# VectorE's chained stages in pieces of one link, and scores over 32 rows at a time, in a two-layer gated stack

## The reference, cut to what matters

```
# x: 16 batches x 256 tokens x 256;  ctx: 16 x 120 x 256
x = x + tanh(g_xattn[0]) * attention_1(layernorm(x), ctx, mask)   # A: 4 heads of 64, rotary
x = x + tanh(g_ffn[0])   * ffn_fp4(layernorm(x))                  # F: blockwise FP4 of input and hidden
x = x + tanh(g_xattn[1]) * attention_2(layernorm(x), ctx, ctx)    # B: 16 heads of 16
x = x + tanh(g_ffn[1])   * moe(layernorm(x))                      # R routes each token to 2 of 8 experts, M runs them

# attention_2, for each batch and head (d_k = 16):
Q, K, V = query @ Wq + bq, key @ Wk + bk, value @ Wv + bv
attn = softmax(Q @ K.T / sqrt(16));  out = concat(attn @ V) @ Wo + bo

# fp4_quant_dequant, for blocks of 16 values:
scale = max(max(|x|) / 6, 1e-12);  q = nearest value of the FP4 grid to x / scale, times scale
```

## Time and profile before

| | us |
|---|---|
| median of 3 runs | 1640.79 |
| lowest, highest | 1635.14, 1644.37 |
| the profiled execution | 1642.42 |
| its span in the trace | 1640.8 |
| PE busy (share of the span) | 1400.4 (85%) |
| DVE busy | 1117.3 (68%) |
| ACT busy | 993.4 (61%) |
| POOL busy | 413.3 (25%) |
| mean granted TensorE clock, share of full speed | 0.949 |

### The profile page before, as it was taken

One profiled execution on the slowest core, in us unless ns is written; L12 is line 12 of the kernel. 1 busy time (PEld: TensorE's weight loads), 2 busy tenths in 40 slices (PEclk: granted clock), 3 DMA queues, 4 the chain that ended last, 5 costly groups with the idle time before them and its releaser, 6 DMA issues.

```text
span 1640.8 us, 35711 instructions
## 1 busy us (share of the span) xinstructions
PE 1400.4 (85%) x11645; PEld 1072.6 (65%) x11646; DVE 1117.3 (68%) x2887; ACT 993.4 (61%) x2861; POOL 413.3 (25%) x560
## 2 busy tenths in 40 slices
PE   2567789989999889989998671999999999999994
PEld 1445556665666566656664430888888888888883
DVE  7977779899988999899986534344444454444452
ACT  1244778888888888888876760444445444455542
POOL 0101011211122211212111112334433444344442
PEclk9587999999999999999999975999999999999997
DMA  6020132112320223203220005551231412322214
GB/s 192 13 87 30 62 103 103 45 61 104 103 92 21 95 104 103 72 33 104 94 94 8 8 14 179 177 162 32 33 112 30 114 32 35 108 35 32 35 31 123
DMA packets 63158, 123.58 MB, mean 75 GB/s; under 512 B 13955, under 2 KB 51967, under 8 KB 58879
## 3 DMA queue, kind: packets, MB, share of 16 engines
q1 hardware_dynamic: 45743, 102.75, 18.0%
q0 software_dynamic: 17312, 19.56, 7.2%
HBM read 78.64 MB, written 48.04 MB: 77 GB/s over the span
## 4 chain that ended last, share of the span: by engine, by line
PE 52%; DVE 32%; ACT 8%; issue 5%; DMA 2%; POOL 1%; SPq 0%; DVEq 0%; ACTq 0%; POOLq 0%
PE bank L1401 15%; PE bank L1403 14%; PE bank L1402 14%; DVE b_mn L1121 4%; ACT b_ex L746 3%; PE bank L1483 2%; PE bank L1495 2%; DVE wm L1238 1%; DVE f_hs L1182 1%; DVE split_room L1265 1%; DVE wm L1190 1%; PE bank L1719 1%; DVE x L1176 1%; DVE wm L1196 1%; DVE wm L1201 1%
## 5 line engine op out<-in xcount | busy, mean ns | idle before, releaser
L1401 PE MATMUL bank<-split_room,wm 128*128 128x256 f16 x1152 | 314.9, 273 | 8.2 <-issue 6.8
L1378 DVE SCALAR_TENSOR_TENSOR split_room<-bank,b12e,split_room 128x256 f32<-128x256 f32 x288 | 138.2, 484 | 265.6 <-ACT split_room L900 260.8
L1402 PE MATMUL bank<-split_room,wm 128*128 128x256 f16 x1152 | 314.8, 273 | 0.0
L1403 PE MATMUL bank<-split_room,wm 128*128 128x256 f16 x1152 | 314.7, 273 | 0.0
L900 ACT ACTIVATE split_room<-bank,b12e 128x256 f32<-128x256 f32 x288 | 134.2, 470 | 196.0 <-PE bank L1403 194.2
L746 ACT ACTIVATE b_ex<-bank,b_mn 128x120 f32<-128x120 f32 x512 | 177.0, 361 | 36.9 <-DVE b_mn L1121 28.0
L1403 PE MATMUL bank<-wm,split_room 128*128 128x256 f16 x576 | 157.0, 273 | 0.0
L1401 PE MATMUL bank<-wm,split_room 128*128 128x256 f16 x576 | 157.0, 273 | 0.0
L1402 PE MATMUL bank<-wm,split_room 128*128 128x256 f16 x576 | 157.0, 273 | 0.0
L692 POOL DMA_INDIRECT acc<-split_room,m_cur x72 | 116.1, 1612 | 133.0 <-ACT split_room L914 106.1
L1483 PE MATMUL bank<-b_k,b_q 128*128 128x480 f32 x256 | 131.8, 597 | 14.6 <-ACT b_q L834 14.6
(11 more groups left out here) (356 smaller groups left out, 3616.3 us busy)
## 6 DMA issues: line engine op xcount, KB each, us to landing
split_room<-in_L_ffn_W SPq DMA_DIRECT2D x48, 512.0 KB, 8.0
wsplit<-split_room SPq DMA_DIRECT2D x16, 1536.0 KB, 6.6
wm<-wsplit SPq DMA_DIRECT2D x16, 1536.0 KB, 8.5
acc<-x SPq DMA_DIRECT2D x17, 256.0 KB, 2.2
xin<-in_x SPq DMA_DIRECT2D x16, 256.0 KB
rows<-r_row SPq DMA_DIRECT2D x16, 256.0 KB, 3.7
ct<-in_ctx SPq DMA_DIRECT2D x16, 120.0 KB
cb<-in_ctx SPq DMA_DIRECT2D x16, 120.0 KB, 2.6
```

Source lines behind the costliest of these rows:

```text
L1378: dve.scalar_tensor_tensor(m_h[:, c % 3], bank[c % 4][:, TILE:2 * TILE], b12e[:, p, 1, c:c + 1], m_s[:, c % 2], ALU.add, ALU.mult).then_in ...
L1401: pe.matmul(o, lh, rh, start=start, stop=False)
L1402: pe.matmul(o, ll, rh, start=False, stop=False)
L1403: return pe.matmul(o, lh, rl, start=False, stop=stop)
```

## The change

1. **DVE's stages are cut at the waits.** `A.ln` becomes `A.ln`, `A.ln_1`, `A.ln_2`, `A.ln_3`; `F.ln`, `B.ln` and `R.ln` become three pieces each, `A.rk`, `A.r0`, `A.r1`, `A.p0` and `A.p1` two each, the FP4 stages eight per part instead of four (three for the input), `R.logit` six, `R.rank` seven. The instructions and their waits stay; the order decides what runs between two pieces.
2. **The scores of B** are made for two rounds at once. Each round is two products over the 32 rows of its group, 240 columns each (`e` is 0 and 1); the four products of two rounds lie in turn over two row groups and two banks. Both rounds may start only when the exponentials of the round before them are done, and the minimum of either waits for both. `b_k` shrinks to `[P, NK, 2, S]`, and ACT writes it with two copies over 128 partitions instead of eight over 32.
3. **For the new place of the heads**, the columns of `wq1`, `wk1` and the bias of the keys are split in eight (four) parts by DVE once, and the bias of the queries is loaded with 8 DMAs instead of 1.
4. **All tables of the order are new.**

```diff
-        b_k = sb("b_k", [P, NK, 2, QUAD, S])
+        b_k = sb("b_k", [P, NK, 2, S])
...
-            sp.dma_start(bqk[:, :], bq.rearrange("(c p) -> p c", p=P), allow_slow_non_contiguous=True).then_inc(wB_in, 16)
+            b_ = bq.rearrange("(c e f a d) -> d c e f a", c=2, e=2, f=2, a=2)
+            for c in range(2):
+                for a in range(2):
+                    for f in range(2):
+                        at = 64 * a + 32 * c + 16 * f
+                        sp.dma_start(bqk[at:at + K1, :], b_[:, c, :, f, a], allow_slow_non_contiguous=True).then_inc(wB_in, 16)
...
-                for j in range(QUAD):
-                    h = slice(PITCH * j, PITCH * (j + 1))
-                    for a in range(2):
-                        last = act.activation(b_k[h, :, a, j], bank[2][h, 0:NK * S].rearrange("p (c s) -> p c s", c=NK), ACT.Copy, scale=C[h, C_M + a:C_M + a + 1])
+                for f in range(2):
+                    last = act.activation(b_k[:, :, f], bank[2][:, 0:NK * S].rearrange("p (c s) -> p c s", c=NK), ACT.Copy, scale=C[:, C_M + f:C_M + f + 1])
...
+                        for c in range(2):
+                            for a in range(2):
+                                for k in range(NK):
+                                    k_ = slice(k, k + 1)
+                                    split(head_order(st1[:, n_ - 1, k_], c, a, True)[:, 0],
+                                          head_order(w[:, 0, k_], c, a, False)[:, 0], head_order(w[:, 1, k_], c, a, False)[:, 0])
...
-                        dve.wait_ge(G.s_mm, b * n + k + 1)
+                        dve.wait_ge(G.s_mm, b * n + (k + 1 if G is A else k // 2 * 2 + 2))
...
+                def pair(b, k0):
+                    if k0 == 0:
+                        pe.wait_ge(B.q, b + 1)
+                        pe.wait_ge(B.k, b + 1)
+                    else:
+                        pe.wait_ge(B.exp, b * n + k0)
+                    for e in range(NK):
+                        for k in (k0, k0 + 1):
+                            t, r = k // per, k % per
+                            h = slice(PITCH * r, PITCH * (r + 1))
+                            last = pe.matmul(sbks[k % 2][:, e * 2 * S:(e + 1) * 2 * S], q[h, e, t * P:(t + 1) * P], kk[h, e], start=True, stop=True)
+                            if e == NK - 1:
+                                last.then_inc(B.s_mm, 1)
...
-                            r = k % per
-                            last = pe.matmul(sbk[:, 0:QUAD * S], q[:, r % 2, t * P:(t + 1) * P], kk[:, r % 2, r // 2], start=True, stop=True)
```

DVE's steady order after the change:

```diff
+            "DVE": ("W1/1 A.ot/0 B.ln/2 B.rx1/3 W2/1 F.gu0/1 A.out/0 A.ln/-1 B.ln_1/2 A.ln_1/-1 B.ln_2/2 F.gu1/1 A.ln_2/-1 B.p7/3 "
+                "F.q0a/1 A.ln_3/-1 B.o1/3 F.q0a_1/1 F.q0a_2/1 F.gu2/1 B.out/3 R.ln/3 R.ln_1/3 R.ln_2/3 B.ct/2 B.zt/2 F.gu3/1 "
+                "F.q0b/1 F.q1a/1 F.q1a_1/1 F.q1a_2/1 F.q0c/1 F.q0c_1/1 B.v/2 A.t/-1 B.s0/2 B.s1/2 F.p0/1 R.t/3 F.p0_1/1 "
+                "F.q1b/1 A.rk/-1 R.logit/3 R.logit_1/3 R.logit_2/3 R.logit_3/3 R.logit_4/3 R.logit_5/3 F.q1c/1 B.s2/2 "
+                "R.rank_0/3 F.q1c_1/1 R.rank_1/3 F.p1/1 B.s3/2 F.p1_1/1 F.ht0/1 A.rk_1/-1 A.r0/-1 A.r0_1/-1 A.r1/-1 A.r1_1/-1 "
+                "B.s4/2 F.ht1/1 B.s5/2 F.ln/0 A.s0/-1 F.ln_1/0 R.rank_2/3 F.ln_2/0 W0/0 B.s6/2 F.qa/0 B.rx0/2 F.qa_1/0 "
+                "F.qa_2/0 F.qb/0 R.rank_3/3 A.s1/-1 F.qc/0 B.p3/2 F.qc_1/0 R.rank_4/3 F.p/0 R.rank_5/3 F.p_1/0 F.d1/1 B.o0/2 "
+                "A.p0/-1 B.s7/2 A.p0_1/-1 A.p1/-1 R.rank/3 A.p1_1/-1 F.t/0").split(),
```

More of the change, by code:

```diff
@@ L401, in gated_stack @@
+            "POOL": ("A.ln@0 A.ln@1 F.ln@0 A.ln@2 F.ln@1 B.ln@0 A.ln@3 F.ln@2 B.ln@1 A.ln@4 R.ln@0 F.ln@3 R.scatter@0 B.ln@2").split(),
[7 rows of a table added]
+                "B.s0@1 B.s1@1 R.logit@0 F.a1@2 B.t0@1 B.s2@1 B.t1@1 F.ht0@2 B.t2@1 B.s3@1 W0@3 F.ht1@2 W1@3 B.t3@1 B.s4@1").split(),
[22 rows of a table added]
+                "B.o0@1 B.s7@1 A.p0_1@4 A.p1@4 R.rank@0 A.p1_1@4 F.t@3").split(),
[8 rows of a table added]
+                "F.ht0@2 A.q0@4 B.t1@1").split(),
         }
         ORDER = {
-            "SP": ("A.load/-1 B.load/1 B.out/3 W/0 R.rank/3").split(),
@@ L444, in gated_stack @@
+            "POOL": ("R.ln@13 B.ln@15 R.scatter@13 R.ln@14 R.scatter@14 R.ln@15 R.scatter@15").split(),
[6 rows of a table added]
+                "B.s7@15 B.t6@15 B.t7@15 B.rx1@15 B.r7@15 B.o1@15 R.z@15 R.t@15 R.logit@15").split(),
[11 rows of a table added]
+                "R.rank_4@15 R.rank_5@15 R.rank@15").split(),
[6 rows of a table added]
+                "B.p4@15 B.t5@15 B.t6@15 B.p5@15 B.t7@15 B.p6@15 B.p7@15 B.out@15 R.t@15 R.logit@15 R.rank@15").split(),
         }
@@ L1130, in stage, with values @@
                         ca.link(dve.reciprocal(rd[:, t], pv[:, :, width]))
+                    return stage
+                def values(k):
+                    def stage(b, p):
+                        t = k // per
+                        pv = pbks[t][:, 0:heads * (width + 1)].rearrange("p (h d) -> p h d", h=heads)
+                        ca.go_on(b)
                         ca.wait()
@@ L1137, in rounds @@
                 if G is A:
-                    made.update({f"{G.name}.p{k}": values(k) for k in range(per - 1, n, per)})
+                    made.update({f"{G.name}.p{k}": shares(k) for k in range(per - 1, n, per)})
+                    made.update({f"{G.name}.p{k}_1": values(k) for k in range(per - 1, n, per)})
                 return made
@@ new lines, in f_scale, with stage, f_inverse @@
+            def f_scale(n):
+                v, m, sc = F_PARTS[n]
+                def stage(b, p):
+                    cf.go_on(b)
+                    cf.wait()
+                    cf.link(dve.tensor_scalar(sc[:, 0], sc[:, 2], SIXTH, 1e-12, ALU.mult, ALU.max))
+                return stage
+            def f_inverse(n):
+                v, m, sc = F_PARTS[n]
+                def stage(b, p):
+                    cf.go_on(b)
+                    cf.wait()
+                    dve.reciprocal(sc[:, 1], sc[:, 0]).then_inc(F.v, 1)
+                return stage
@@ new lines, in f_scaled, with stage, f_grid @@
+            def f_scaled(n):
+                v, m, sc = F_PARTS[n]
+                def stage(b, p):
+                    dve.wait_ge(F.v, b * 3 + n + 1)
+                    dve.tensor_tensor(blocks(v), blocks(v), over(sc[:, 1], BLK), ALU.mult).then_inc(F.u, 1)
+                return stage
+            def f_grid(n):
+                v, m, sc = F_PARTS[n]
+                def stage(b, p):
+                    dve.wait_ge(F.abs, b * 3 + n + 1)
+                    dve.tensor_scalar(m, m, 1.5, STEP, ALU.max, ALU.mult).then_inc(F.m, 1)
+                return stage
@@ new lines, in f_round, with stage, f_unshift @@
+            def f_round(n):
+                v, m, sc = F_PARTS[n]
+                def stage(b, p):
+                    dve.wait_ge(F.m, b * 3 + n + 1)
+                    dve.scalar_tensor_tensor(v, v, BELOW, m, ALU.mult, ALU.add).then_inc(F.t, 1)
+                return stage
+            def f_unshift(n):
+                v, m, sc = F_PARTS[n]
+                def stage(b, p):
+                    cf.go_on(b)
+                    dve.wait_ge(F.t, b * 3 + n + 1)
+                    cf.link(dve.tensor_tensor(v, v, m, ALU.subtract))
+                return stage
@@ L1228, in f_q, with f_unscale, stage @@
+            def f_unscale(n):
+                v, m, sc = F_PARTS[n]
+                def stage(b, p):
+                    cf.go_on(b)
+                    cf.wait()
+                    dve.tensor_tensor(blocks(v), blocks(v), over(sc[:, 0], BLK), ALU.mult).then_inc(F.hq, 1)
                 return stage
@@ L1336, in _ @@
             stages.update({f"F.gu{k}": f_gu(k) for k in range(4)})
-            stages.update({f"F.q{t}{x}": f_q(t, part) for t in range(NT)
-                           for x, part in zip("abc", (quantise_a, quantise_b, quantise_c))})
+            for G, ch, source in ((F, cf, A), (B, cb_, F), (R, cr, B)):
+                name = {F: "F.ln", B: "B.ln", R: "R.ln"}[G]
+                stages[name], stages[name + "_1"], stages[name + "_2"] = variances(G, ch, source)
+            for n_ in range(3):
+                w_ = ("", "0", "1")[n_]
+                for x, make in (("a", f_largest), ("a_1", f_scale), ("a_2", f_inverse), ("b", f_scaled), ("c", f_grid), ("c_1", f_round)):
+                    stages[f"F.q{w_}{x}"] = make(n_)
+                stages[f"F.p{w_}"], stages[f"F.p{w_}_1"] = f_unshift(n_), f_unscale(n_)
             steps("DVE", stages)
```

183 lines of the change are left out of this document (97 added, 86 removed), and 121 rows, old and new, of tables (FIRST, LAST, ORDER).

## The result

The changed kernel takes 1648.73 us (median; 1643.82 to 1651.93), the kernel before 1638.36 beside it. The ratio is 1.0057, with a 95% interval of 1.0044 to 1.007. The profiled execution has a span of 1648.4 us against 1640.8, and a mean granted TensorE clock of 0.897 against 0.949. Forecast were 1597 us, 1578 to 1630, so the result lies outside the range and on the other side.

A forecast was written before the change was run, and what follows sets the result against it. VectorE (DVE) was taken as the bound, with a beat of 52.24 us. Twelve beats at -3.0 (-36), fill +2, drain -5 and seam -5 gave -44 us from 1642.4, a median of 1597 us, range 1578 to 1630.

The forecast's parts named there:

- 34 places ... 3.0 us per batch go: VectorE's steady step: 34 dependent neighbours and 5 holds cost 5.2 us, the new order 2.2, so 3.0 us less per batch.
- 1.0 us per pair: B's scores on TensorE: two row groups overlap, so a pair takes 1.0 us against 1.62, changes of array shape included.
- rival (a): B's scores: row groups don't overlap, TensorE gets 0.8 us more per batch, beat 50.6, total 1619 us; chance 0.11.
- Nothing excludes that the new order costs waits elsewhere: VectorE's steady step: caveat on the saved links, giving bounds of 0 and 4.5 us per batch; 3.0 was taken.
- Rival (b): Steady part: the gain hides in moved cross waits, beat falls by 1 us only, 1628 us, or 1640 at nothing; chance 0.17.
- Less PE buys slack and no time of its own: B's scores: 2.0 us less TensorE work per batch, but TensorE is not the bound, so no time is gained directly.
- 3.9 us a round and 7.7 for two: Drain, B.15 alone: the old rounds form a ring, read from scores at 959.38 and again at 963.24.
- The term of 2.1 us saved per pair: Drain: two rounds as a pair take 5.6 us against 7.7; three to four pairs save some 7, drain taken as -5.
- The fill: Start, first batches: preparation +7 us, lost links -4.5, net rounded to +2, bounds -4 and +8.
- The splits' +7: Preparation on VectorE: smaller weight splits +5.5 us and the keys' bias +1.5, together +7 in the fill.
- the store is out of the way: Seam: early weight splits free the last scatter from the store and give VectorE its tables sooner, -5 us, bounds 0 and -9.
- Rival (c): Ring of banks 2 and 3 closes: exponentials and scores can't overlap, beat 1.8 us longer, 1661 us, slower; chance 0.08.

The follow-up runs named there:

- with the clock held: Changed kernel plus 13 products per batch that nobody reads, put where TensorE has only small work: ratio 1.0004 to the kernel before.
- the two runs with scores over 128 rows: Changed kernel with 128-row scores, old keys tile and preparation: 1.0398; kernel before with only VectorE's stages cut and interleaved by hand: 1.0438.
- old order: Changed kernel, its scores over 32 rows kept, with all order tables of the kernel before and VectorE's pieces next to each other: ratio 1.055.
- 128 rows: Changed kernel with its new orders, but scores over 128 rows and the old keys' tile, copies and preparation: ratio 1.0398.
- pieces alone: Kernel before (its scores and other engines' orders) with only VectorE's stages cut and its steady order interleaved by hand: ratio 1.0438.
- rounds apart: Changed kernel with the two rounds of B's scores taken apart: in all sixteen batches 1.0523, in batches 14 and 15 alone 1.0114.
- scatter moved: Changed kernel with GpSimd's scatter later in its steady order, behind B.ln and the next A.ln: ratio 1.0253.
- the first four experiments: Not numbered in the text; told first are old orders 1.055, 128-row scores 1.0398, 13 unread products 1.0004 and these in the kernel before 1.0021.
- the run with the store moved: Changed kernel with SyncE's store of the last split weights issued behind batch 13's output: ratio 1.0221, run again on another chip 1.0077.

## Why the prediction was wrong, point by point

- **"34 places ... 3.0 us per batch go"** was right in size: 2.8, of which 2.3 are pauses and overlaps, as counted, and 0.5 shorter durations, which were not. The keys' copies too: 20 take 7.9 us, 0.8 per batch. In this view of ScalarE's groups they answer to the earlier trace rows:

```profile
L847 ACT ACTIVATE b_k<-bank,C 128x240 f32<-128x240 f32 x20 | 7.9, 442 | 0.0
```

- **The scores' "1.0 us per pair"** was right, and rival (a) is out. The row groups start 7 ns apart:

```profile
442.42 1.08 PE L1602 MATMUL bank<-b_k,b_q 32*128 32x240 f32 x8 [0.38 <-ACT b_q L855]
443.43 0.66 PE L1786 MATMUL bank<-C,r_z 128*128 128x128 f32 x4
```

  From 442.42 to 443.43 is 1.01 us: four slots of 0.20 and 0.1 at entry and at exit. The page "TensorEngine Tiling (Array Packing)" of the Trainium skill, "Key Properties", says that a change of mode drains the engine; the 0.1 us at either end agree with it.
- **"Nothing excludes that the new order costs waits elsewhere", and 3.0 taken all the same: this step failed.** The forecast carried the long waits over unchanged. They grew from 2.4 to 3.65 us; with the clock held they are 2.8. So of the 1.25 the falls made 0.8 and the order 0.4. Rival (b), a gain hidden by moved waits, describes this best: the beat fell by 1.5. The beat came out 1.6 us above 49.2; ten beats are 15 us of the miss.
- **"Less PE buys slack and no time of its own"** is where the fall of the clock was missed. Shorter, lighter work on TensorE is not slack alone: its granted clock fell behind a stretch in which it was busy 6.4 of 8 us with, among others, scores over 32 rows, transposes, and logits of 8 columns. It fell in the two runs with scores over 128 rows too, for 3.1 and 8.2 us per batch, where the long waits were 7.4 and 13.3: light work is one way into such a stretch, waiting another. The forecast had no term for it; the earlier trace rows show none in the steady part, but the trace of before has 0.76 from 936 to 997 us, around, and this was not read as a warning.
- **The drain, "3.9 us a round and 7.7 for two"**, misread. Between 959.38 and 963.24 lie two products for one bank, but the other bank's round runs between others in the same ring: six rounds took 16.1 us there from first to seventh minimum, 5.4 for two. Against my 5.6 for a pair no gain was left even at the full clock, and the one clean lap at that clock is 1.0 us longer than before (4.89 against 3.86). As run, mostly at the half clock, it is 21.4 us for three pairs, 7.1 each. The term of 2.1 us saved per pair is the step that failed here. The stretch was forecast at -11 and came at +16.7, 28 of the 52 us of the miss.
- **The fill** was forecast +2 within -4 and +8, and is +4.4. The order of batch 0, put back, gave at most 1.1 of it. The splits' +7 is borne out at F of batch 0 (5 to 7 us); what was missing is the new orders' own 7 to 9 there, and that later stages take most of both up.
- **The seam, "the store is out of the way"**, failed in its reading of queues: VectorE splits early, but SyncE's place for the store was not moved. It is issued at 1001.50, as late as before, and the last scatter lands 10.4 us behind its issue:

```profile
1001.50 5.48 DMA wsplit<-split_room
...
1008.55 0.95 POOL slots L655
1009.50 10.43 issue
...
1020.68 2.21 DMA m_ids<-slots
```

  Moving it gains 1.5 to 1.8 us, not 5.
- **Rival (c)** named the sign. Its mechanism, exponentials and scores that can't overlap, is there in the ring of batch 15 at 1.0 us in the lap above. For the steady part it isn't shown: taking the pairs apart made it slower still, but also took away what a pair saves on TensorE.

By stretches the miss of 51.6 us is 2.4 (fill) + 15.4 (beat) + 27.7 (drain) + 6.1 (seam).

## What to carry to other kernels

Add up the pauses an order removes, but treat the waits between engines as a result of the whole order: in five partial versions (old order, 128 rows, pieces alone, rounds apart, scatter moved) they were four to eleven us per batch longer than before, far beyond any pause. When a change makes the work of TensorE lighter, or makes it wait, look at where its clock may fall and cost the neighbours at half speed. Compare such runs on one chip: here the chip alone moved the beat by 0.8 us and more. And read a ring of two banks by the distance between the same event some rounds apart, not by one lap.

## What the hardware showed that was not expected

**A clock that falls in an engine 93% busy.** Thirteen products nobody reads made the beat shorter by 0.9 us on one chip and 0.6 on another.

**A signal that comes late, by the chip.** In the changed kernel TensorE transposes A's output while GpSimd issues four indirect transfers. Where the result was taken, and on the chip of the first four experiments, its signal reaches ScalarE 0.01 us behind the last transposition; on two others it comes 1.8 us late in nearly every batch, and on two more 2.6. First ScalarE in the trace of the result, then the run with the store moved on the last kind, and there GpSimd and TensorE:

```profile
322.68 0.60 ACT L788 ACTIVATE a_zt<-bank 128x512 f16<-128x512 f32 x1
```

```profile
324.76 0.60 ACT L790 ACTIVATE a_zt<-bank 128x512 f16<-128x512 f32 x1 [2.69 <-remote]
...
321.49 0.95 POOL L657 DMA_INDIRECT slots<-r_pair,r_at  x1 [0.30 <-issue]
322.75 1.11 POOL L657 DMA_INDIRECT slots<-r_pair,r_at  x1 [0.30 <-issue]
...
321.35 0.66 PE L1680 MATMUL bank<-C,a_z 128*128 128x128 f32 x4
...
325.99 0.67 PE L1637 MATMUL bank<-C,b_ex 128*120 128x128 f32 x4 [2.08 <-ACT b_pt L779]
```

The transposes end at 322.01, TensorE's next signals all come together from 324.65 on, and TensorE itself then stands still for 2.08 us. With it goes a beat of 51.6 us instead of 50.8 for the same kernel, and a ratio of 1.0085 instead of 1.0057. In batches 0 to 4 it is absent on every chip. With the scatter moved away the signal came at 0.01 us on a chip where the two kernels beside it had 1.5 and 1.8. So the overlap with the indirect transfers brings it about. What holds the signal, and why chips differ, stays open.

**Left open:** what the other 6 us of batches 13 and 14 are, whether an order found for the old scores with these pieces would keep the clock up, and what the whole drain would take at the full clock without added products.
